# The diagonal of the pair products by ones, behind level 0, in a delta-rule attention kernel

## The reference, cut to what matters

```python
q = _short_conv(hidden_states @ Wq, conv_q).reshape(B, T, H, DK)
k = _short_conv(hidden_states @ Wk, conv_k).reshape(B, T, H, DK)
v = _short_conv(hidden_states @ Wv, conv_v).reshape(B, T, H, DV)
q = _l2norm(q) * SCALE
k = _l2norm(k)
...
beta = jax.nn.sigmoid(hidden_states @ Wb)
def step(S, inp):
    qt, kt, vt, gt, bt = inp
    S = S * jnp.exp(gt)[..., None]
    err = jnp.einsum('bhk,bhkv->bhv', kt, S)
    delta = bt[..., None] * (vt - err)
    S = S + kt[..., None] * delta[:, :, None, :]
    ot = jnp.einsum('bhk,bhkv->bhv', qt, S)
    return (S, ot)
```

## Time and profile before

| | us |
|---|---|
| median of 3 runs | 6108.75 |
| lowest and highest run | 6107.04, 6117.89 |
| profiled execution | 6114.65 |
| its span | 6112.9 |

### The profile page before, as it was taken

How to read it: one execution, slowest core, us unless ns; L and a number is a source line. 1 busy time by engine, 2 the same in 40 slices (tenths; PEclk the granted TensorE clock), 3 DMA queues, 4 the chain that set the end, 5 groups by cost and what they waited for, 6 DMA issues and landing times. The chain is left out here.

```text
span 6112.9 us, 92718 instructions
## 1 busy us (share of the span) xinstructions
PE 5887.2 (96%) x33208; PEld 4267.3 (70%) x33208; DVE 4404.6 (72%) x7563; ACT 3050.3 (50%) x5133; POOL 1806.4 (30%) x1636
## 2 busy tenths in 40 slices
PE   5699999999999999999999999999999999899999
PEld 2477777777777777777777777777777777544444
DVE  7788888888888888888888888888888888311110
ACT  2455555555555555555555555555555555301101
POOL 2233333333333333333333333333333333100000
PEclk8899999999999999999999999999999999899999
DMA  2101111111011111111011111110101111231221
GB/s 83 38 22 35 29 35 29 35 28 34 26 32 29 35 28 31 33 28 34 26 33 28 35 28 35 28 35 27 31 27 35 29 28 28 69 106 62 80 78 47
DMA packets 183711, 236.04 MB, mean 39 GB/s; under 512 B 25048, under 2 KB 128088, under 8 KB 179168
## 3 DMA queue, kind: packets, MB, share of 16 engines
q1 hardware_dynamic: 111072, 188.22, 10.3%
q10 hardware_dynamic: 72192, 41.95, 2.2%
HBM read 183.75 MB, written 46.38 MB: 38 GB/s over the span
## 5 line engine op out<-in xcount | busy, mean ns | idle before, releaser
L632 PE MATMUL bank<-xT,weights 128*128 128x512 f32 x4096 | 2160.1, 615 | 29.6 <-PEq L153 29.6
L1264 POOL TENSOR_TENSOR KR<-KR,decay_u 128x256 f32<-128x256 f32 x896 | 910.4, 1016 | 3048.9 <-PE bank L658 3048.9
L896 DVE SCALAR_TENSOR_TENSOR conv<-pre,taps,conv 128x512 f32<-128x512 f32 x1152 | 1082.0, 948 | 18.0 <-ACT conv L1104 8.9
L911 DVE TENSOR_TENSOR KQ<-KQ,decay_u 128x512 f32<-128x512 f32 x896 | 695.3, 776 | 497.1 <-PE bank L658 496.7
L658 PEld LDWEIGHTS bank<-KQ,KR 128*128 128x128 f32 x7168 | 905.8, 191 | 188.5 <-issue 181.4
L658 PE MATMUL bank<-KQ,KR 128*128 128x128 f32 x7168 | 962.5, 277 | 4.3 <-DVE KQ L911 3.2
L931 DVE COPY_PREDICATED all_pairs<-level_mask,bank 128x512 f32<-128x512 int32 x896 | 795.0, 887 | 0.0
L632 PEld LDWEIGHTS bank<-xT,weights 128*128 128x128 f32 x4096 | 663.3, 192 | 184.0 <-issue 161.2
L1149 ACT ACTIVATE T_inv<-bank 128x256 fp32r<-128x256 f32 x640 | 250.0, 391 | 956.7 <-PE bank L700 956.7
L681 PEld LDWEIGHTS bank<-T_inv,pairs 128*128 128x128 f32 x3072 | 464.9, 192 | 366.8 <-issue 333.1
L681 PE MATMUL bank<-T_inv,pairs 128*128 128x64 f32 x3072 | 713.9, 358 | 0.7 <-DVE T_inv L947 0.5
(11 more groups left out here) (160 smaller groups left out, 8701.9 us busy)
## 6 DMA issues: line engine op xcount, KB each, us to landing
decay_u<-decay_scratch SPq DMA_DIRECT2D x128, 510.0 KB
beta_u<-beta_scratch SPq DMA_DIRECT2D x128, 256.0 KB
y_scratch<-y_rn ACTq DMA_DIRECT2D x128, 256.0 KB, 2.3
y_in<-y_scratch SPq DMA_DIRECT2D x32, 1024.0 KB, 4.8
xt<-in_L_attn_hidden_states SPq DMA_DIRECT2D x8, 1024.0 KB, 5.2
x_in<-in_L_attn_hidden_states SPq DMA_DIRECT2D x32, 256.0 KB, 5.0
out<-o_out ACTq DMA_DIRECT2D x32, 256.0 KB, 2.0
w<-in_L_ffn_W SPq DMA_DIRECT2D x8, 704.0 KB, 5.0
```

What stands on the lines that cost most here:

```text
L632: last = nc.tensor.matmul(bank[w % 2][:], weights[par][:, w, k, :], xT[:, k, u % J * UC:(u % J + 1) * UC], start=k == 0, stop=k == KC - 1)
L896: nc.vector.scalar_tensor_tensor(conv[:, w], pre[:, w, :, t:t + P], taps[par][:, w, t:t + 1], conv[:, w], ALU.mult, ALU.add).then_inc(step ...
L911: nc.vector.tensor_tensor(second_halves, second_halves, pair[:, :, 0:1].unsqueeze(1).to_broadcast([P, 2, blocks, 1 << l]), ALU.mult).then_ ...
L1264: nc.gpsimd.tensor_tensor(first_halves, first_halves, second.to_broadcast([P, UC >> (l + 1), 1 << l]), ALU.mult).then_inc(keys_scaled.sem, 1)
```

## The change

The four products of the diagonal go. In their place GpSimd multiplies `KR` and `q_hat` element by element into `rnorm[:, 1]` (`diagonal_product`), ScalarE rounds that to F32R into `squares[:, 1]` (`round_diagonal`, behind `silu_v`), GpSimd subtracts the rounded part (`diagonal_left`, into `squares_rest[:, 1]`), and TensorE sums both over the channels with two F32R products with ones into bank 4. All rows of bank 4 then hold the diagonal, and `keep_diagonal` takes it under the identity as before. On TensorE `diagonal()` moves behind `refine(c, 1)`, on VectorE `keep_diagonal` behind `take_residual(c, 1)`. GpSimd does both its parts ahead of `scale_keys(0)`.

```diff
@@ TensorE
             def diagonal():
                 if m is None:
                     return
-                wait(pe, unit_ready, m, 1)
+                wait(pe, diag_rest_ready, m, 1)
                 if b is not None:
                     wait(pe, k_rows_ready, b, 1)
-                for i in range(B):
-                    last = nc.tensor.matmul(bank[4][:, cols(i)], KR[:, cols(i)], q_hat[:, cols(i)], start=True, stop=True)
-                last.then_inc(diag_done.sem, 1)
+                nc.tensor.matmul(bank[4][:], ones_r[:], squares[:, 1, :], start=True, stop=False)
+                nc.tensor.matmul(bank[4][:], ones_r[:], squares_rest[:, 1, :], start=False, stop=True).then_inc(diag_done.sem, 1)
...
-                    wait(pe, pairs_ready, m, l)
+                    wait(pe, pairs_ready, m, max(l, 2))
...
             project(2, (2,))
-            diagonal()
             level(0)
             inverse_xt(1)
             refine(c, 1)
+            diagonal()
             project(2, (3,))
             inverse_z(2)
             level(1)
@@ VectorE
                 wait_apart(dve, diag_done.sem, diag_done.at(m, 1), dve_waits_passed)
-                if b is not None:
-                    wait_apart(dve, pairs_kept.sem, pairs_kept.at(b, 1), dve_waits_passed)
+                wait_apart(dve, pairs_ready.sem, pairs_ready.at(m, 1), dve_waits_passed)
...
-                wait_apart(dve, pairs_ready.sem, pairs_ready.at(m, l + 1), dve_waits_passed)
+                if l >= 1:
+                    wait_apart(dve, pairs_ready.sem, pairs_ready.at(m, l + 1), dve_waits_passed)
+                elif b is not None:
+                    wait_apart(dve, pairs_kept.sem, pairs_kept.at(b, 1), dve_waits_passed)
...
             add_identity_to_z(1)
-            keep_diagonal()
             scale(0)
             keep_pairs(0)
             normalised_output()
             take_residual(c, 1)
+            keep_diagonal()
             add_identity_to_z(2)
@@ ScalarE
+                if w == 1 and m is not None:
+                    wait(act, diag_done, m, 1)
                 nc.scalar.activation(squares[:, w], silu[:, w], ACT.Square).then_inc(squares_ready.sem, 1)
+
+            def round_diagonal():
+                if m is None:
+                    return
+                wait(act, sums_done, m, 2)
+                wait(act, diag_product_ready, m, 1)
+                nc.scalar.activation(squares[:, 1], rnorm[:, 1], ACT.Copy).then_inc(diag_rounded.sem, 1)
...
+                if w == 1 and m is not None:
+                    wait(act, diag_rest_ready, m, 1)
                 nc.scalar.activation(rnorm[:, w], bank[2][:], ACT.Ln, bias=l2_eps[:, 0:1]).then_inc(sums_taken.sem, 1)
...
             silu_v()
+            round_diagonal()
             take_t(1)
@@ GpSimd
+        def diagonal_product(u):
+            wait_apart(pool, unit_ready.sem, unit_ready.at(u, 1), pool_waits_passed)
+            nc.gpsimd.tensor_tensor(rnorm[:, 1], KR[:], q_hat, ALU.mult).then_inc(diag_product_ready.sem, 1)
+
+        def diagonal_left(u):
+            wait_apart(pool, diag_product_ready.sem, diag_product_ready.at(u, 1), pool_waits_passed)
+            wait_apart(pool, diag_rounded.sem, diag_rounded.at(u, 1), pool_waits_passed)
+            nc.gpsimd.tensor_tensor(squares_rest[:, 1], rnorm[:, 1], squares[:, 1], ALU.subtract).then_inc(diag_rest_ready.sem, 1)
...
+            diagonal_product(s.m)
+            diagonal_left(s.m)
             for l in range(LEVELS):
```

More of the change, by code:

```diff
@@ L467, in attention @@
     diag_done = signal("diag_done", 1)
+    diag_product_ready = signal("diag_product_ready", 1)
+    diag_rounded = signal("diag_rounded", 1)
+    diag_rest_ready = signal("diag_rest_ready", 1)
     level_done = signal("level_done", LEVELS)
```

## The result

| | before | changed |
|---|---|---|
| median | 6108.66 us (4 runs) | 6204.71 us (4 runs) |
| lowest, highest | 6107.04, 6117.89 | 6202.91, 6207.15 |
| span of the profiled execution | 6112.9 | 6201.3 |

The changed kernel takes 1.0154 times as long, with a 95% interval of 1.0137 to 1.0172. The forecast was 6193 us in a range of 6148 to 6240. By the spans, 88.4 us were added over 128 steps, 0.69 us a step; by the medians 96 us, 0.75 us a step. In the traces, from 500 to 4800 us, the mean step is 39.33 us before and 40.04 us after, 0.71 more (the 39.36 of the earlier trace rows is that of most steps; one in eight lasts 39.13).

What follows compares the result with a forecast made beforehand. TensorE's instruction list plus its waits bounds each step. Level 1 waiting for VectorE's list costs 0.41 us and the collision 0.25; 128 x 0.66 = 84 us on 6108.75 gives 6193 us, range 6148 to 6240.

Steps and rivals of the forecast that it cites:

- What bounds the kernel: Whole step: TensorE's instruction list in order plus its waits, 39.36 us; matmul time saved is gained, any new wait lost.
- What TensorE gives back: Diagonal on TensorE: four fp32 products of 0.89 us become a pair of 0.52, 0.37 us shorter a step without waits.
- What VectorE must do first: Ahead of level 1: keep_diagonal stands last in 4.08 us of VectorE's list, so level 1 starts 0.41 us later.
- The collision: VectorE's normalised_output meets GpSimd's scale_keys(0) and ends at 20.73 in place of 20.48, 0.25 us more.
- its upper bound: Level 1 start: 0.85 us later in all, if the subtraction runs to 19.6 and scale_keys(0) to 20.3.
- The sign "0.9 to 1.0 us": Trace after, on VectorE: normalised_output would take 0.9 to 1.0 us in place of 0.74.
- TensorE didn't wait for it before either: Level 1: VectorE, 0.55 us behind GpSimd before, is now first, but TensorE had not waited for it, so no gain.
- The wait ahead of the diagonal: TensorE reaches the diagonal at 19.25, the rest comes at 19.46; about 0.2 us, hidden in level 1's wait.
- The one without collision: Rival at normalised_output: no collision, only VectorE's order counts, 0.41 x 128 = 52 us, 6161 us; chance 0.22.
- GpSimd went first: Rival at level 0: subtraction starts before scale(0), which waits about 1.15 us; level 1 1.56 later, 6308 us; chance 0.10.
- the third: Rival: level 0's predicated copy falls from 1.31 to 0.73 us with GpSimd elsewhere; 6093 or 6062 us; chance 0.08.
- The fourth: Rival: the later 0.57 us wait behind add_identity_to_z shrinks by what level 1 loses, about 6110 us; chance 0.05.

Runs made afterwards that it cites:

- the first three experiments: Changed kernel with keep_diagonal ahead of normalised_output, 6125.98 us; changed kernel without GpSimd's subtraction, 6158.75 us; kernel before with only diagonal and copy moved, 6156.93 us.

## Why the prediction was right, point by point

With 8.60 us taken off its times, the changed kernel's level 0 stands where the forecast had it (16.56):

| step | forecast | measured |
|---|---|---|
| `scale(0)` starts | 17.65 | 17.67 |
| GpSimd's subtraction starts, ends | 17.9 to 18.0, 19.46 | 17.82, 19.50 |
| `scale_keys(0)` ends | 20.17 | 20.30 |
| `normalised_output` starts, ends | 19.74, 20.73 | 19.75, 20.85 |
| `keep_diagonal` ends | 21.98 | 22.08 |
| level 1 starts | 22.03 | 22.23 |
| later than before | 0.66 | 0.86 |
| made good later | 0 | 0.14 |

- *What bounds the kernel* held: the 0.72 of the last two rows times 128 is 92 us, against 88 between the spans, 96 between the medians and 0.71 x 128 = 91 by the mean steps. The forecast had a step of 40.0 us, and it is 40.04.
- *What TensorE gives back* was 0.32 to 0.34 us and not 0.37: the pair takes 0.57 where it stands behind a wait, 0.55 behind none. As forecast it isn't seen, since VectorE sets level 1.
- *What VectorE must do first*, 0.41 us, is the run with the move alone: level 1 stands 5.32 - 0.89 - 3.92 = 0.51 us later there. The 0.10 between is TensorE's start: 0.14 us behind the end of the copy there (43.77 to 43.91), where I had taken 0.05 from the wait at `inverse_xt(5)`; the copy itself ends 5.18 us behind level 0's start, and 5.17 was forecast.
- *The collision* was 0.36 us and not 0.25, near its upper bound: with `scale_keys(0)` to 20.3 the prediction's own sum gives 0.38 (20.86 less 20.48), so 0.79 in all and not the 0.85 that it states. The measured 0.86, with TensorE's later start in it, lies just above either bound. The run without the subtraction has the collision apart: 46 us for 128 steps, 0.36 each. The term was mis-sized by `scale_keys(0)`, which takes 0.80 us where I had 0.71 (19.50 to 20.30). The 0.71 is right where it stands behind VectorE's product (4.66 to 5.38 in the run without the subtraction); behind GpSimd's own subtraction it is longer, and why was not settled. The sign "0.9 to 1.0 us" for `normalised_output` missed for the same reason: it took 1.10.
- *"TensorE didn't wait for it before either"* was wrong. Before, `inverse_xt(3)` stood 0.94 us behind level 2, and 0.81 in the changed kernel. VectorE's `add_identity_to_z(3)` ended 0.06 us before that start, so TensorE did wait, 0.13 us, too short for a row of the waits. In the changed kernel VectorE is first at level 1 (0.69 us for its `KQ` product in place of 1.24) and that wait is gone. The two errors, 0.20 more at level 1 and 0.14 less at level 2, nearly cancel: that the step came out so close to 0.66 is in part luck.
- *The wait ahead of the diagonal* was there (0.38 us where 0.2 was forecast) and free, as the run without the subtraction shows.
- *The rivals.* The one without collision is the run without the subtraction, 6158.75 against the 6161 it was given. GpSimd went first in the run with the work alone, where the rounding comes at the same time and level 0 is 0.89 later; in the changed kernel VectorE was 0.15 us ahead, a thin margin. Level 0's predicated copy took 1.31 us in every kernel, also with GpSimd elsewhere, which rules out the third. The fourth had the wait of the earlier trace rows shrink; it kept its length (1.72 us from level 4 to `inverse_xt(5)` in most steps of both kernels), and what was made good, 0.14, lay at level 2.

The Trainium skill's rule of exclusion (page "SBUF — State Buffer", section "Who interferes with whom") held in the rows shown here: `normalised_output` beside `scale_keys(0)` 1.10 us, apart from it 0.75.

## What to carry to other kernels

Ask of a moved step which later step needs it, and walk the whole list in front of it on the engine that does it: two products less on TensorE were worth nothing while the copy of their result stood sixth on VectorE and the next product needed its bank. A result that is wanted late should go to a bank that is wanted late, and the work that makes it belongs where its engine waits anyway; with the same two products with ones the kernel took 1.5% more or 1.2% less than before, by their bank and place alone. Work beside the bound is free or not by who waits for what it disturbs: the same collision cost 46 us in the changed kernel and next to nothing with the diagonal in bank 6. And compare starts, not only the rows of waits: 0.13 us in each step had no row, and was 17 us.

## What the runs showed of the hardware

- A copy of 128x12 on VectorE, SBUF to SBUF, took 0.96 us in place of 0.16 when GpSimd's product of 128x512 had started before it (changed kernel and the run with the work alone). TensorE didn't wait for it: in the kernel before, VectorE idled for 0.44 us ahead of the `add_identity_to_z(1)` that follows, and the delay fell into that. Timeline of the changed kernel:

```profile
3022.90 1.27 POOL L1297 TENSOR_TENSOR rnorm<-KR,silu 128x512 f32<-128x512 f32 x1 [5.52 <-DVE KQ L1032]
...
3023.24 0.96 DVE L885 COPY pre<-pre 128x12 f32<-128x12 f32 x1
```

- TensorE began 0.14 to 0.15 us behind the end of the copy it waited for ahead of level 1 (the changed kernel and the first three experiments), but 0.05 behind the end of VectorE's instruction ahead of `inverse_xt(5)`. What makes the difference was not settled.
- The predicated copies of level 0 and 1 take 1.29 to 1.34 us and those of the other levels 0.70 to 0.75, in every run and with GpSimd busy or idle. They copy pieces of 1 and 2 elements (`1 << l`), the others pieces of 4 and more; no run varied that alone.
